# Second sum's statistics on ScalarE, rounded input's transposes ahead of the wide layer's last products

## The reference

```
x = x + tanh(g_xattn[0]) * pruned_attention(layernorm(x), ctx)          # 16 heads, keeps 460 of 512 keys
x = x + tanh(g_ffn[0])   * fp4_gated_mlp(layernorm(x))                  # 256 -> 2 x 704 -> 256, blocks of 16 rounded to 4 bits
x = x + tanh(g_xattn[1]) * layernorm(linear_attention(ctx, n) + n)      # n = layernorm(x)
x = x + tanh(g_ffn[1])   * int8_linear(x)                               # x rounded per token to 127 steps
layernorm: (x - mean) / sqrt(var + 1e-5) over the 256 features
```

## Time and profile before

| what | value |
|---|---|
| time, median of 3 runs | 1225.81 us (1225.57 to 1227.15) |
| the profiled execution's own time | 1224.68 us |
| its span in the trace | 1222.6 us |
| PE busy | 1010.4 us (83%) |
| DVE busy | 1015.9 us (83%) |
| ACT busy | 935.4 us (77%) |
| POOL busy | 163.4 us (13%) |
| chain that ended last | PE 44%, ACT 38%, issue 9%, DVE 7% |

### The profile page before, as it was taken

The page is one execution under the profiler, slowest core; times in us unless marked ns, Lnnn a source line. Parts: engine busy times, 40 slices in busy tenths (PEclk is TensorE's granted clock), DMA queues, the critical chain, the costliest instruction groups (busy, mean ns, idle before and its releaser), DMA issues.

```text
span 1222.6 us, 18004 instructions
## 1 busy us (share of the span) xinstructions
PE 1010.4 (83%) x5688; PEld 485.7 (40%) x5688; DVE 1015.9 (83%) x2009; ACT 935.4 (77%) x2135; POOL 163.4 (13%) x183
## 2 busy tenths in 40 slices
PE   6888999977677777777777768888999999999974
PEld 5655566521111111111111112235677777767652
DVE  5887677788889888888988886457999999999955
ACT  5455665489999999999999997676567767766734
POOL 2221231020000000000000000101132222221212
PEclk9899999989999999999999999889999999999985
DMA  9730553042111222120123201101111111110001
GB/s 303 167 122 6 198 135 117 19 122 45 32 32 28 44 44 45 35 42 19 41 44 79 46 6 36 35 9 40 52 35 35 62 43 35 58 38 27 21 15 35
DMA packets 77906, 71.80 MB, mean 59 GB/s; under 512 B 13754, under 2 KB 71412, under 8 KB 77812
## 3 DMA queue, kind: packets, MB, share of 16 engines
q1 hardware_dynamic: 77812, 70.65, 21.9%
HBM read 42.83 MB, written 27.28 MB: 57 GB/s over the span
## 4 chain that ended last, share of the span: by engine, by line
PE 44%; ACT 38%; issue 9%; DVE 7%; SPq 1%; DMA 1%; POOL 0%; ACTq 0%; DVEq 0%
ACT ea L1318 18%; ACT prob L1332 15%; PE ps_a L1595 13%; PE ps_b L1553 8%; PE ps_v L1553 3%; PE ps_c L1568 2%; PE ps_a L1604 2%; DVE nmax L1219 2%; PE ps_c L1629 1%; PE ps_b L756 1%; PE ps_v L1191 1%; PE ps_c L1175 1%; PE ps_b L731 1%; PE ps_v L697 1%; PE ps_b L1142 1%
## 5 line engine op out<-in xcount | busy, mean ns | idle before, releaser
L1318 ACT ACTIVATE ea<-ps_a,nmax 128x512 f32<-128x512 f32 x512 | 361.5, 744 | 68.4 <-DVE nmax L1219 68.3
L1219 DVE TENSOR_REDUCE nmax<-ps_a 128x2 f32<-128x1024 f32 x256 | 313.7, 1225 | 52.3 <-PE ps_a L1142 51.0
L1332 ACT ACTIVATE prob<-ps_b 128x1024 f32<-128x1024 f32 x214 | 235.2, 1099 | 0.0
L1142 PE MATMUL ps_b<-q_st,k_st 52*128 52x512 f16 x512 | 106.0, 391 | 136.3 <-ACT prob L1332 124.4
L1142 PEld LDWEIGHTS ps_b<-q_st,k_st 52*128 52x128 f16 x512 | 26.2, 93 | 363.8 <-ACT prob L1332 303.1
L1595 PE MATMUL ps_a<-wgu,xT 128*128 128x352 f32 x512 | 166.5, 466 | 4.9 <-ACT xT L1758 3.7
L1191 PE MATMUL ps_v<-prob,v_in 128*16 128x512 f32 x1024 | 135.8, 602 | 11.7 <-DVE att L1286 11.7
L1175 PE MATMUL ps_c<-ea,rz 128*32 128x512 f32 x1024 | 138.1, 612 | 0.0
L1318 ACT ACTIVATION_READ_ACCUMULATOR ea<-ps_a,nmax 128x1 f32 x512 | 134.2, 262 | 0.0
L1595 PEld LDWEIGHTS ps_a<-wgu,xT 128*128 128x128 f32 x512 | 92.9, 191 | 50.4 <-issue 6.6
L1770 ACT ACTIVATE ea<-ps_a 128x352 f32<-128x352 f32 x128 | 59.6, 466 | 59.3 <-PE ps_a L1595 59.1
(11 more groups left out here) (279 smaller groups left out, 1707.4 us busy)
## 6 DMA issues: line engine op xcount, KB each, us to landing
k_scr<-k_p SPq DMA_DIRECT2D x24, 256.0 KB, 2.9
q_scr<-q_p SPq DMA_DIRECT2D x24, 256.0 KB, 2.6
q_st<-q_scr SPq DMA_DIRECT2D x32, 192.0 KB, 4.7
k_st<-k_scr SPq DMA_DIRECT2D x32, 192.0 KB, 5.1
c_in<-in_ctx SPq DMA_DIRECT2D x8, 512.0 KB, 4.5
x_in<-in_x SPq DMA_DIRECT2D x8, 512.0 KB, 5.5
v_scr<-v_s SPq DMA_DIRECT2D x8, 512.0 KB, 3.2
v_in<-v_scr SPq DMA_DIRECT2D x16, 256.0 KB, 3.2
```

The costliest lines, as they stand in the source:

```text
L1142: return e.matmul(bank, left[b][o:o + rows, r, t * P:t * P + P], right[b][o:o + rows, r], start=True, stop=True)
L1219: e.tensor_reduce(nmax[u % 2][:, t].rearrange("p (h r) -> p r h", h=2)[:, r], ps_a[:, z % 2 * 2:z % 2 * 2 + 2], AX_X, ALU.max, negate=True ...
L1318: e.activation(ea[c % RING][:, g % 4], ps_a[:, g % 4], ACT.Exp, bias=nmax[u % 2][:, t, n:n + 1], accum_out=tot[u % 2][:, t, n:n + 1]).then ...
L1332: e.activation(dst, ps_b[:, :, :], ACT.Exp).then_inc(s_prob, 1)
```

## The change

The second sum's mean and variance are no longer made by VectorE in turns 2 to 15 (bn_stats, bn_aggr), but by ScalarE, in a new function second_stats behind h_magnitude: two Copy activations with an accumulator (the mean), then two Square activations with an accumulator (the squares about that mean), which wait for the Copies. VectorE's ve_b is made in two instructions, slot 1 (the third layernorm's) and slot 0 (the second sum's, which waits for the second half of second_stats), and the two stand between the two roundings of the hidden row, behind output. roots_b comes behind the second rounding, as before. In turns 16 and 17 the statistics stay on VectorE. GpSimd's first_bias waits for hq where it waited for r2. TensorE transposes q8 ahead of the third part of down instead of behind it.

```
@@ gpsimd
             if unit(i + 1) is not None:
                 if i >= 2:
-                    e.wait_ge(s_dve_r2, i - 1)
+                    e.wait_ge(s_dve_hq, i)
                 first_bias(i + 1)
@@ tensor, turn
                 e.wait_ge(s_act_hT, 3 * u1 + 2)
                 down(u1, 1)
-                e.wait_ge(s_act_hT, 3 * u1 + 3)
-                down(u1, 2).then_inc(s_pe_down, 1)
             if u4 is not None:
...
                 ins.then_inc(s_pe_q8T, 1)
+            if u1 is not None:
+                e.wait_ge(s_act_hT, 3 * u1 + 3)
+                down(u1, 2).then_inc(s_pe_down, 1)
@@ scalar
+        def second_stats(u, i):
+            e.wait_ge(s_dve_r2, u + 1)
+            e.wait_ge(s_nb_b, i)
+            for t in range(N):
+                ins = e.activation(sq[:, t], r2[:, t], ACT.Copy, scale=1.0 / D, accum_out=mv_b[:, 0, t, 0:1])
+            ins.then_inc(s_act_st2, 1)
+            e.wait_ge(s_act_st2, 2 * u + 1)
+            e.wait_ge(s_ve_b, i)
+            for t in range(N):
+                ins = e.activation(sq[:, t], r2[:, t], ACT.Square, scale=-1.0, bias=mv_b[:, 0, t, 0:1],
+                                   accum_out=mv_b[:, 0, t, 1:2])
+            ins.then_inc(s_act_st2, 1)
...
                 h_magnitude(u1)
+            if u2 is not None and i < UNITS:
+                second_stats(u2, i)
@@ vector
+        def second_sum(i):
+
+            u2 = unit(i - 2)
+            if u2 is not None:
+                residual(u2)
+                if i >= UNITS:
+                    stats(lambda t: r2[:, t], mv_b, 2, 0).then_inc(*dv.up())
+                    e.wait_ge(*dv.now())
+
         def variances_b(i):
             u2, u3 = unit(i - 2), unit(i - 3)
-            if u2 is not None:
-                residual(u2)
-                stats(lambda t: r2[:, t], mv_b, 2, 0).then_inc(s_dve_st2, 1)
-                e.wait_ge(s_dve_st2, u2 + 1)
             if u3 is not None:
                 e.wait_ge(s_act_sq, u3 + 1)
-            e.tensor_scalar(ve_b[i % 2][:, :, :], mv_b[:, :, :, 1], LN_EPS, None, ALU.add).then_inc(s_ve_b, 1)
+            v, mv = ve_b[i % 2], mv_b[:, :, :, 1]
+            if u2 is None or i >= UNITS:
+                e.tensor_scalar(v[:, :, :], mv, LN_EPS, None, ALU.add).then_inc(s_ve_b, 1)
+            else:
+                e.tensor_scalar(v[:, 1], mv[:, 1], LN_EPS, None, ALU.add).then_inc(*dv.up())
+                e.wait_ge(s_act_st2, 2 * u2 + 2)
+                e.tensor_scalar(v[:, 0], mv[:, 0], 1.0 / D, LN_EPS, ALU.mult, ALU.add).then_inc(s_ve_b, 1)
@@ vector, round_blocks
             if between is not None:
-                roots_b(between)
+                between()
             e.wait_ge(*dv.now())
@@ vector, turn
-            if i < TURNS_B:
-                variances_b(i)
+            second_sum(i)
             if u0 is not None and u5 is not None:
                 output(u5)
-            if u1 is not None:
-                h_round(u1, UNITS if i == UNITS else None)
-            if i < TURNS_B and i != UNITS:
+            if i < UNITS:
+                h_round(u1, lambda: variances_b(i))
                 roots_b(i)
+            elif i < TURNS_B:
+                variances_b(i)
+                if u1 is not None:
+                    h_round(u1, lambda: roots_b(i))
+                else:
+                    roots_b(i)
```

More of the change, by code:

```diff
@@ L1433, in feed @@
         m.sem(f"act_{n}3") for n in ("xn", "xm", "xT", "hm", "dec", "decT", "sq", "z", "n4", "q8T"))
-    (s_dve_r1, s_dve_r2, s_dve_xq, s_dve_x, s_dve_hid, s_dve_hq, s_dve_h, s_dve_st2, s_dve_zg, s_dve_r4,
+    (s_dve_r1, s_dve_r2, s_dve_xq, s_dve_x, s_dve_hid, s_dve_hq, s_dve_h, s_dve_zg, s_dve_r4,
      s_dve_q, s_dve_out) = (m.sem(f"dve_{n}3") for n in (
-         "r1", "r2", "xq", "x", "hid", "hq", "h", "st2", "zg", "r4", "q", "out"))
+         "r1", "r2", "xq", "x", "hid", "hq", "h", "zg", "r4", "q", "out"))
     s_pe_gu, s_act_gu = m.sem("pe_gu3"), m.sem("act_gu3")
     s_pe_hT, s_act_hT = m.sem("pe_hT"), m.sem("act_hT")
-    s_act_st1 = m.sem("act_st13")
+    s_act_st1, s_act_st2 = m.sem("act_st13"), m.sem("act_st23")
     s_act_sil = m.sem("act_sil3")
```

## The result

The changed kernel took 1229.56 us (median of 9 runs, 1226.46 to 1231.41) against 1225.81 for the kernel before (9 runs in the same rounds): a ratio of 1.0029, 95% interval 1.0018 to 1.0040, 0.3% slower. The prediction was 1229.7. The profiled execution took 1229.4 us, with a span of 1227.7.

What follows compares the result with a forecast made beforehand. The prediction took PE's loop (23.53 us) to bound steady feed turns, DVE's 0.1 us behind. Its terms 1.5 (turn 2), 1.8 (turns 3, 4), 0.3 (steady) and 0.27 (last) made +3.87 us: 1229.7, range 1220.6 to 1231.3.

Steps and rivals of the forecast that it cites:

- The bound: Steady feed turns: PE's loop of 23.53 us sets the period, DVE's about 23.42, so relieving one alone gains little.
- rival (a): GpSimd's power on ve_b isn't held up, PE's 23.20 us sets steady turns: about 1220.7 us; chance 22 in 100.
- When ve_b is ready: ScalarE's statistics chain releases DVE, and ve_b's slot 0 starts, at E + 3.38 us.
- E: The end of h_over in a turn, the moment from which the prediction counts its times.
- The power: GpSimd's power on ve_b begins inside the second rounding and takes 2.32 us, not 1.02; roots_b starts at E + 5.97.
- Steady turns: Turns 5 to 14: roots_b 0.11 us later, 0.08 regained, so +0.03 us a turn, 23.56 us, DVE's loop.
- ten periods: +0.3: Sum over steady turns 5 to 14: +0.3 us, range -1 to +1.5.
- rival (c): Steady loop worse: z, first_mean, first_squares bound by nb_b, PE's gate product by ScalarE's copy; +0.15 us a turn, 1231.2; 8 in 100.
- Turns 2 to 4: Early feed turns, set by DVE: turn 2 +1.5 us including third_bias's collision, turns 3 and 4 +0.90 each.
- rival (b): The power is held up but turns 2 to 4 absorb most of their delay: 1226.4 to 1228 us; 15 in 100.
- Turns 15 to 17: Last feed turns: roots_b +0.16 in turn 15 and -0.35 in turn 16, down +0.23 in each; together +0.27 us.
- The sum: All terms: 1.5 + 1.8 + 0.3 + 0.27 = +3.87 us on 1225.81, forecast 1229.7 us, 0.3% slower.

Runs made afterwards that it cites:

- relieving PE alone: Kernel before with only q8's transposes moved ahead of down's third part, statistics left on VectorE: 1227.95 us, ratio 1.0013.
- kernels with room for the power: Changed kernel plus useless VectorE work between slot 0 and the second rounding: a 0.40 us reduction (1223.45 us) or a two-operand addition (1223.8 us).
- the long reduction: Changed kernel plus a useless one-input reduction of 128 x 4 x 120 between slot 0 and the second rounding, turns 2 to 15: 1223.45 us, ratio 0.9974.
- the addition: Changed kernel plus a useless VectorE addition of two SBUF pieces of r2 between slot 0 and the second rounding: 1223.8 us, ratio 0.9983.
- the short reduction: Changed kernel with statistics on VectorE in turns 2 to 4 and, from turn 5, a useless 128 x 4 x 60 reduction behind slot 0: 1229.4 us, ratio 1.0026.
- kernel with the statistics alone: Changed kernel with TensorE's old order, q8's transposes behind down's third part: 1232.72 us, ratio 1.0052.
- second profile of before: The kernel before, unchanged, run and profiled once more as control: 1224.43 us, ratio 1.0007.
- am's reduction moved: Changed kernel with the last layernorm's largest value taken between slot 0 and the second rounding in turns 4 to 15: 1228.26 us, ratio 1.0032.
- turn 3's addition behind nb_a: Changed kernel with GpSimd's third_bias of turn 3 put behind its power of ve_a and nb_a: 1229.55 us, ratio 1.0026.

## Why the prediction was right, step by step

**The bound.** Right. DVE and PE stood 0.1 us apart, and relieving PE alone gave 0.08 us a turn (23.53 to 23.45). DVE's loop had been put at 23.42. PE's loop after the change had been put at 23.20, by the lower end of what the transposes bring; it is shorter, since the kernels with room for the power turn in 23.06 to 23.18 and PE still waits for DVE in them. In the changed kernel this is hidden; rival (a) was priced with the 23.20.

**When ve_b is ready.** Right to 0.01 us: E + 3.37, predicted E + 3.38. The pricing of the four activations by their twins held: from 1105.29 to the end of the last read at 1107.32 are 2.03 us. first_bias cost nothing, as predicted: it ran from 1104.05 to 1105.33, and the first rounding, from 1105.50, took its 1.62.

**The power.** This was the step that decided, and it was right in kind and size: 2.32 us, ending 0.88 after the rounding, roots_b at E + 5.97 as predicted. The row that carried it was one of two in which the power followed a rounding at the same distance, among seventeen of 1.02 us. That it was this mechanism and not another is shown by the kernels with work in between: the same program with 0.40 us more in a turn is 0.48 us a turn faster. Rival (a) fell. Its condition, slot 0 more than 0.25 us ahead of the rounding, was a little short: the long reduction puts 0.39 us between them (1125.92 and 1126.31), the addition 0.36, and both let the power in; the short reduction, with 0.26 (1103.25 and 1103.51), doesn't.

**Steady turns.** +0.06 us in place of +0.03 each. By the count from E: nb_b +0.12, ve_a's slot 0 +0.04 (1115.80, E + 11.82, against E + 11.78), the next E +0.04. Over eight turns this makes 0.23 us more than predicted. The larger miss, 0.35, is in the first two of the ten. Before, turns 5 and 6 took 23.46 and not 23.53: PE's longer loop had not caught up with DVE yet, so nothing was there to be relieved (last_product started 0.35 us ahead of residual in turn 5, 0.28 in turn 6, then 0.20 and 0.19). And in turn 5 of the changed kernel output, without the statistics ahead of it, waited for a last product that wasn't done:

```profile
916.16 0.88 DVE L2082 SCALAR_TENSOR_TENSOR o_b<-ps_c,sc,r 128x256 f32<-128x256 f32 x2 [0.47 <-DVE r L1950]
```

The term "ten periods: +0.3" measured +0.88; ten equal periods was the main wrong step. I had removed 1.11 us between residual and output and never asked what output itself waits for. The kernel with the statistics alone shows that wait in every turn. Of rival (c) the waits came, z for nb_b (5.2 us in ten turns) and PE's gate product for ScalarE's copy (2.9), but the turn grew by 0.03 us beyond the forecast, not by 0.15.

**Turns 2 to 4.** +0.92 and +0.93 for a predicted +0.90. Turn 2: +1.27 for +1.50; the collision was there (1.23 us, predicted 1.24), but only 0.74 of its 1.1 us reached the next residual. Of rival (b) that is the part that came true; the rest of it fell, since nothing of turns 3 and 4 was made up. Without the collision turn 2 takes 24.25 us, 0.53 more than before, where 0.4 had been worked out.

**Turns 15 to 17.** Turn 15 +0.46 for +0.39. In turn 16 roots_b started 4.41 us behind residual, predicted 4.39. Turn 16 to 17 had been put at -0.12 (-0.35 and +0.23). It took 20.91 us, against 20.96 in the second profile of before, but 22.55 in the recorded one. There a run of 24 products took

```profile
1181.76 6.99 PE L1553 MATMUL ps_b<-wdn,hT 128*128 128x256 f32 x24
```

and 5.93 us in the second profile. Beside the recorded profile of before, the changed kernel thus seems to win 1.6 us in turn 16 that the change has no part in.

**The sum.** Up to turn 16 the feed lost 4.46 us where 3.99 had been predicted; the medians differ by 3.75. The agreement of 1229.56 with 1229.7 to 0.14 us is partly luck: +0.58 in the ten steady turns was missed and -0.23 in turn 2 went the other way, and the 0.7 us between 4.46 and 3.75 are assigned to nothing. A total can't be told to better than about a microsecond here; the interval of the ratio reaches from 2.2 to 4.9 us.

## What to carry to other kernels

When work is taken off an engine, list what stood behind it in time, on the other engines too: here 1.11 us of statistics on VectorE had covered the end of a last product on TensorE; and list what now comes later: ve_b, which had been ready ahead of output and both roundings, with the power hidden behind them, came between the two roundings. A small GpSimd instruction between two dependent VectorE steps should find VectorE in an instruction with one SBUF operand as it asks for its data; a fraction of a microsecond of order decides over 1.3 us. And moving a piece of cover only pays if its old place didn't need it.

## What the runs showed of the hardware

- A power of 128 x 4 on GpSimd took 1.02 us beside a reduction, 1.06 when it began 0.19 us before the end of a two-operand addition, 2.32 and 2.51 when a rounding of 1.62 us, which reads two operands, ran 0.15 us behind its start.
- Two two-operand instructions of VectorE back to back did not keep GpSimd out through both: by the time of its end (0.87 us behind the end of the first) it went in between them, and the second took no longer (1.62 us).
- An addition of 128x512 on GpSimd (1.27 us) that began 0.06 us ahead of a two-operand step of 128x4 on VectorE held this step to its own end: 1.23 us in place of 0.16.
- In each of the fourteen profiles TensorE's granted clock fell during the idle of turn 16 or within some 3 us of its end. How long it stayed low differed between executions of one kernel: in the recorded profile of before it was 0.50 from 1175 to 1181 us and 0.82 in the next 8, in the second one 0.55 from 1176 to 1182 and 1.00 in the next 8.

```profile
1181.00:1189.00 8.00, 8.00 (x33) 5.77 (x31) 0.32 (x2) 2.43 (x8) 0.00 (x0) 0.82 0.07 23
```

```profile
1182.00:1190.00 8.00, 7.20 (x36) 5.28 (x36) 1.74 (x7) 4.15 (x13) 0.12 (x1) 1.00 0.10 34
```

That goes with the 1.6 us of turn 16: turn 16 to 17 took 22.55 us in the recorded profile of before and 22.8 in two other kernels (am's reduction moved, and turn 3's addition behind nb_a), whose clock was 0.83 to 0.84 in the corresponding 8 us; in the eleven other profiles it took 20.3 to 21.2, with a clock of 1.00 there. The two levels are 1.2 and 2.4 GHz, so 0.50 is the lower one throughout.
